# A branch on the weights' low parts is moved behind the first four gate products of a fused attention and feed-forward kernel

## What is computed

```python
x = x + attn_a(layernorm(x))
x = x + ffn(layernorm(x))
x = x + attn_b(layernorm(x))
x = x + ffn(layernorm(x))

def _tlin(x, w, s):
    return jnp.einsum('bsi,oi->bso', x, w) * s
h = silu(_tlin(x, w1_w, w1_s)) * _tlin(x, w2_w, w2_s)
h = gelu(_tlin(h, h1_w, h1_s))
h = gelu(_tlin(h, h2_w, h2_s))
return _tlin(h, w3_w, w3_s)
```

## Time and profile before

| | us |
|---|---|
| median of three executions | 714.45 |
| profiled execution, its time | 717.27 |
| profiled execution, its span | 715.5 |
| TensorE busy with products | 657.6 (92%) |
| VectorE busy | 497.8 (70%) |
| ScalarE busy | 450.6 (63%) |
| GpSimd busy | 425.5 (59%) |

### The profile page before, as it was taken

One profiled execution on the slowest core, in us unless ns is written; L12 is line 12 of the kernel. 1 busy time (PEld: TensorE's weight loads), 2 busy tenths in 40 slices (PEclk: granted clock), 3 DMA queues, 4 the chain that ended last, 5 costly groups with the idle time before them and its releaser, 6 DMA issues.

```text
span 715.5 us, 14025 instructions
## 1 busy us (share of the span) xinstructions
PE 657.6 (92%) x4713; PEld 457.9 (64%) x4716; DVE 497.8 (70%) x958; ACT 450.6 (63%) x801; POOL 425.5 (59%) x443
## 2 busy tenths in 40 slices
PE   3789998689999999997999999998989999999997
PEld 1455555477777877665555555554546777787785
DVE  6769998665657768556788888885678566775521
ACT  3668887446566666545676677775765556566664
POOL 4544543267777786633345645653666777778673
PEclk9989999899999999999999999998999999999999
DMA  6101230000000000560457666663221000000000
GB/s 195 41 22 42 53 42 2 1 1 1 1 0 0 0 1 2 162 245 7 149 186 235 210 211 225 231 205 137 77 80 47 1 15 16 15 0 15 16 16 29
DMA packets 33028, 52.47 MB, mean 73 GB/s; under 512 B 4560, under 2 KB 9680, under 8 KB 32976
## 3 DMA queue, kind: packets, MB, share of 16 engines
q1 hardware_dynamic: 32784, 51.53, 23.0%
q10 hardware_dynamic: 192, 0.26, 0.1%
HBM read 27.15 MB, written 24.38 MB: 72 GB/s over the span
## 4 chain that ended last, share of the span: by engine, by line
PE 63%; DVE 14%; ACT 8%; issue 7%; DMA 4%; POOL 1%; SPq 1%; DVEq 0%; ACTq 0%; POOLq 0%
PE banks L220 60%; ACT b_prob L1525 4%; DVE xn L182 2%; DVE a_mx L652 2%; ACT a_prob L553 2%; DMA f_h_lo<-b_k_dram 2%; DMA b_o_dram<-b_o 1%; PE banks L212 1%; DVE f_gate L1088 1%; DMA b_k_dram<-b_k_lo 1%; DVE f_h_hi L1091 1%; PE banks L977 1%; DVE f_hidden L1094 1%; DVE a_prob L666 1%; ACT f_g_hi L1044 1%
## 5 line engine op out<-in xcount | busy, mean ns | idle before, releaser
L1158 POOL TENSOR_TENSOR f_g_lo<-f_gelu,f_g_hi 128x512 fp32r<-128x512 f32 x127 | 162.9, 1291 | 54.0 <-ACT f_g_hi L1044 53.4
L1043 ACT ACTIVATE f_gelu<-banks,cols 128x512 f32<-128x512 f32 x128 | 88.3, 690 | 130.6 <-PE banks L220 108.6
L1624 DVE TENSOR_REDUCE b_segment_max<-banks 128x6 f32<-128x768 f32 x128 | 120.2, 950 | 31.1 <-PE banks L220 30.4
L1741 POOL TENSOR_SCALAR_AFFINE_SELECT b_prob<-b_prob 128x512 f32<-128x512 f32 x128 | 81.6, 638 | 93.5 <-ACT b_prob L1525 92.8
L220 PE MATMUL banks<-f_g_hi,whi 128*128 128x512 f32 x320 | 130.2, 407 | 1.9 <-POOL f_g_lo L1158 1.4
L220 PE MATMUL banks<-f_g_lo,whi 128*128 128x512 f32 x320 | 126.7, 396 | 0.0
L1525 ACT ACTIVATE b_prob<-banks 128x768 f32<-128x768 f32 x128 | 102.4, 807 | 38.5 <-PE banks L220 38.2
L1151 POOL TENSOR_TENSOR f_h_lo<-f_hidden,f_h_hi 128x512 fp32r<-128x512 f32 x60 | 77.5, 1292 | 64.5 <-DVE f_hidden L1094 62.8
L220 PE MATMUL banks<-f_h_hi,whi 128*128 128x512 f32 x256 | 104.5, 408 | 5.4 <-POOL f_h_lo L1151 2.7
L220 PE MATMUL banks<-f_h_lo,whi 128*128 128x512 f32 x256 | 101.7, 397 | 0.0
L1044 ACT ACTIVATE f_g_hi<-banks,cols 128x512 fp32r<-128x512 f32 x128 | 87.4, 683 | 0.0
(11 more groups left out here) (125 smaller groups left out, 1093.6 us busy)
## 6 DMA issues: line engine op xcount, KB each, us to landing
f_h_hi<-b_q_dram SPq DMA_DIRECT2D x16, 512.0 KB, 4.0
f_h_lo<-b_k_dram SPq DMA_DIRECT2D x16, 512.0 KB, 5.0
b_o_dram<-b_o SPq DMA_DIRECT2D x8, 1024.0 KB, 4.4
b_q_dram<-b_q_hi SPq DMA_DIRECT2D x16, 256.0 KB, 3.2
b_k_dram<-b_k_hi SPq DMA_DIRECT2D x16, 256.0 KB, 3.0
w_stage<-in_wF SPq DMA_DIRECT2D x8, 352.0 KB, 3.3
b_q_dram<-b_q_lo SPq DMA_DIRECT2D x8, 256.0 KB, 3.6
b_k_dram<-b_k_lo SPq DMA_DIRECT2D x8, 256.0 KB, 3.2
```

The lines of the kernel that those rows point to most:

```text
L1043: nc.scalar.activation(gf[c % 2][:, :], z_bank[c % 2], ACT.Gelu, scale=scale).then_inc(s_gf, 1)
L1158: nc.gpsimd.tensor_tensor(lo[:, c, :], gf[c % 2][:, :], hi[:, c, :].bitcast(F32), ALU.subtract).then_inc(s_glo[c % 2], 1)
L1624: nc.vector.reduce_max(seg[:, g, s, 2 * p:2 * p + 2, :], first_pass[:, 2 * p:2 * p + 2, 0:3 * P].rearrange("p b (c k) -> p b c k", c=3), A ...
L1741: nc.gpsimd.affine_select(out=pr, in_=pr, compare_op=ALU.is_ge, fill=0.0, base=0, pattern=[[0, 4], [1, P]], channel_multiplier=-1).then_in ...
```

## The change

The load of the flag and the branch go behind gate 3 of block 0. All that TensorE does between the old place and the new one stands ahead of the branch, once, and its gates take three terms (`GENERAL`). A wait for the low parts of the weights is put at the head of `pe_last`.

```diff
@@ pe_program
                 run_inner(pe, pe_body)
-                ffn["pe_load_flag"](pe)
                 pe_scores(pe, LAST_BLOCK, 1)
@@ pe_last
                 nxt = link["next"]
+                pe.wait_ge(ffn["s_lo"], ffn["n"])
                 pe_pv(pe, LAST_BLOCK, 0)
@@ pe_load_flag
-        ffn["pe_load_flag"] = pe_load_flag
-
@@ block.tensor
             def from_first_attention(parts):
-                attention_first["pe_last"](pe, parts)
                 ffn_first["pe_blocks"](pe, parts)
...
             attention_first["pe"](pe)
+            attention_first["pe_last"](pe, GENERAL)
+            pe_load_flag(pe)
             pe_either(pe, from_first_attention)
```

## The result

The changed kernel takes 708.88 us, the median of ten executions from 708.16 to 710.31, against 714.0 us for ten executions of the kernel before. The ratio is 0.9931, with a 95% interval from 0.9905 to 0.9958: 3.0 to 6.8 us faster. In two later comparisons it was 0.9954 (0.9934 to 0.9974) and 0.9937 (0.9907 to 0.9967). The forecast was 711.6 us and a gain of 2.85 us, with a range down to 709.4. The sign came out right; the gain is larger than forecast, and the time just outside the range.

A forecast was written before the change was run, and what follows sets the result against it. TensorE, busy 92%, was taken as the bound, with a 2.65 us issue hole at the branch. Chunk 1 gains of 2.2 and 3.4 us gave 2.85 as their middle: 714.45 - 2.85 = 711.6 us, range 709.4 to 713.5.

The forecast's parts named there:

- the border: From the scores of sequence 1 to the start of hidden chunk 1: forecast 2.85 us shorter.
- hidden chunk 1: Second chunk of the hidden product: start forecast at 145.0 or 146.2 us, against 148.44 before.
- the middle case: At the border, TensorE's clock low for 3.4 us from 139.7: chunk 1 at 145.0, a gain of 3.4 us.
- the sequencer stops at a waiting product: At gate 3, sequencer waits for release, not the product's end; load starts at 134.6 us, branch at 135.5.
- the length is a fetch of code: At the far branch, 3.79 us explained by fetching a target over 2,000 instructions on; no row showed it.
- It lies 2.8 us above the median of the runs: Profiled execution, 717.27 us before: its 2.85 us gain was carried unchanged to the median, giving 711.6 us.
- From chunk 1 on everything keeps its distance: Behind the border, TensorE sets the pace, so the 2.85 us gain carries through to the end.
- The wait for queued work: Rival at the branch: part of its 3.79 us awaits an empty queue; 0.8 to 0.9 us more gained, 710.7; chance 0.18.
- The second stall: Rival behind the jump, in hidden chunk 0: sequencer runs dry for another 3.8 us, 716.0 us; chance 0.06.
- Absorbed: Rival behind the border: work with its own pace, above all second-attention transfers, swallows the gain; 714.4 us, chance 0.14.

The follow-up runs named there:

- early load: Changed kernel with the flag's load back at its old place ahead of the scores, only the branch behind gate 3: 709.09 us on average.
- later branch: Changed kernel with the flag's load at its old place and the branch moved behind hidden chunk 0, six more added terms: 711.31 us.
- whole dead block: Kernel before with 128 never-executed matmuls (256 instructions) at the head of the three-term copy: 713.65 us, ratio 0.9988; later 713.67 us on average.
- the table above: Average times, code at old then new place: branch old 714.08 and 710.66 us, branch new 712.68 and 709.96 us; dead code shifted the executed copy.
- with the code shifted back: Changed kernel with 44 never-executed matmuls (88 instructions) at the head of the three-term copy: 713.62 us, ratio 0.9984.
- near copy: Kernel before with its two copies swapped, the two-term copy that runs right behind the branch: 708.69 us on average, later 709.10 us.
- the old branch with its code at the new place: Kernel before with 84 never-executed matmuls at the head of the three-term copy: 710.3 us median, ratio 0.9945; 710.66 us over all executions.

## Why the prediction was right and wrong

**Right: how each step of the border moves.** Counted from the scores of sequence 1, with 1.13 us taken off the forecast's times of day:

| | forecast | measured |
|---|---|---|
| tanh 0 | 127.2 | 127.36 |
| tanh 1 | 130.6 | 130.65 |
| gate 3 | 133.5 | 133.60 |
| tanh 2 | 133.5 | 133.49 |
| branch starts | 134.4 | 134.6 |
| branch, length | 3.79 | 3.51 |
| first hidden product | 138.6 | 138.26 |
| hidden chunk 1 | 143.9 or 145.1 | 144.67 |

Chunk 1 lies at the late end, since the clock stayed low until 144.2 us and not for the 3.4 us of the middle case. That the sequencer stops at a waiting product, and that the branch holds it for its whole length wherever it is taken, stood the tests of the early load (branch and gate 3 together) and of the later branch. That the length is a fetch of code, which no row of before showed, is now seen in the packet of code inside each far branch.

**Wrong in size: the border, 2.85 us.** The step that failed is the one that set the sum against a single trace, "It lies 2.8 us above the median of the runs; the change in the median should be the same". The two low-clock stretches of that trace do not stand in every execution. From the scores to the first transpose of y, six traces with the branch at the old place have 59.5, 59.0, 58.9, 59.4 and, in two without a fall of the clock, 56.0 and 55.9 us. Five with the branch at the new place have 56.8, 57.9, 57.9, 55.7 and 58.1, and in all of them the clock fell. Where the clock was low for the same 10.2 us in all, the old place has 58.9 to 59.5 and the new one 57.9 to 58.1: some 1.2 us are the move's own in the traces, and the rest of the 2.64 us is the clock of two single traces. The mean granted clock from 120 to 160 us is the column behind the five busy times, in the first trace of before and in one of the old branch without a fall (the kernel with a whole dead block, second run):

```profile
120.00:160.00 40.00, 31.40 (x143) 23.01 (x144) 26.12 (x59) 21.04 (x46) 16.39 (x15) 0.87 0.01 1
```

```profile
120.00:160.00 40.00, 31.27 (x159) 23.19 (x158) 27.86 (x59) 22.19 (x46) 18.64 (x17) 1.00 0.00 1
```

The averages are 58.1 and 57.3 us, a difference of 0.8; the timed runs say 0.7 to 1.4 over all chips and less than can be told on one. The change trades a hole of 2.65 us, behind which the clock mostly falls, for one of 3 us, behind which it always fell here.

**Missed altogether: the place of the code.** This is the step that put the time outside the range: the sum has nothing for what follows chunk 1, and the place of the code there is worth 2.7 to 3.4 us by the table above. The failing sentence is "From chunk 1 on everything keeps its distance, as TensorE sets the pace there". It holds as far as it was read, to 285 us. In the second attention the chain goes through transfers, and there a fetch of code may stand in the way of one. The change takes the border's instructions out of the second copy, and so what follows stands some 88 instructions further forward against the blocks. Between the same two ScalarE instructions at 472 and 534 us of the changed trace, five traces with the code at the old place take 1.9 to 2.3 us longer than it, and four with the code at the new place within 0.4 us of it. The first trace of before takes 4.7 longer, since there the clock fell too: from 486 to 493 us its mean was 0.51.

The two stretched transfers, the load at 472 to 485 us and the store at 500 to 511 us, give all of the 1.9 to 2.3 us: between and behind them the five traces lose nothing on the changed one. The timed runs say 2.7 to 3.4 us. For the remainder falls of the clock stand ready, which longer waits may invite. With the branch old the granted clock of the timed executions supports it: 0.986 on average at the old place and 0.990 at the new, which is some 5 us more at the half clock, and 10.2 us at the half clock made the border 3.3 us longer above. With the branch new the clocks are 0.988 and 0.989, too near each other to tell. That the waits cause the falls is argued, not shown.

That the sign was right is so in part luck: most of the measured gain comes from an effect that the prediction didn't have, and with the code shifted back the same change gained 0.16%, not clear of zero.

**The rivals.** The wait for queued work has fallen (early load, late branch: 3.36 and 3.62 us with a full queue). The second stall did not come. "Absorbed" was wrong in its sign: the transfers of the second attention, its very example, added to the gain. The Trainium skill's Advanced Engine Details and Errata, Control Flow Timing, has about 108 ns for a compare-and-branch. The traces agree in size for a branch that isn't taken (71 ns) and for the loop's (76 to 232 ns), and not for the far one of this kernel.

**A better version.** The kernel before with its two copies swapped takes 708.69 and 709.10 us on average, against 708.97, 710.35 and 710.39 for the changed kernel, at ratios of 0.993 and 0.9925 to before. It has no added terms and no hole, and equals the kernel without a branch, 708.76, within what can be told. Swapping the copies also moves the code that runs against the blocks, and its 1 MB store takes 4.7 us, so its 5 us over before are not the hole's alone: against the old branch with its code at the new place, 710.66, it leads by 1.7 ± 0.4 us. The lead over the changed kernel, some 1 us over all runs, is from different chips and not compared side by side.

## What to carry to other kernels

Put the branch's likely side right behind it; a taken branch to far code held TensorE's sequencer for 3.3 to 3.8 us wherever it stood. Before a gain of half a per cent is credited to an edit, shift the executed code by dead instructions without it: here that alone moved the time by 2 to 4 us. And set a sum of this size against several traces, since a fall of the clock in one of them is as large as the effect.

## What was not expected of the hardware

One packet of code, 16 KB, lengthened a 1 MB store from 4.7 to between 5.6 and 6.3 us when it fell among its packets, a load of 512 KB from between 4.7 and 5.3 to between 5.7 and 6.3 us, and a store of 256 KB from 3.8 to 4.8 us. Not every packet does: in the near copy's first trace one started 0.9 us before the end of that load, which took 4.8 us. The stretched store ends when its slowest part does, as its trickle of 14 to 28 GB/s shows.
